# A different order for the four groups of transposes inside each slot of a fused scan kernel

## The reference

```python
proj = xn @ W_in.T;  x, gate = split(proj)            # 2048 channels each
x = silu(conv4(x));  dt, B, C = projections of x      # 16 states per channel
state = state * exp(dt * A) + (dt * x)[..., None] * B # for each token
y = einsum('bdn,bn->bd', state, C)                    # sum over the 16 states
s = ((y + x * D) * silu(gate)) @ W_out.T
g = silu(qlinear(silu(qlinear(xn, gate)) * qlinear(xn, up), down))
out = x_in + s * g
```

## Time and profile before

| | |
|---|---|
| median of 3 runs | 2763.37 us (2761.09 to 2766.05) |
| profiled execution, its own time | 2765.08 us |
| profiled execution, span | 2763.3 us |
| TensorE busy | 2658.4 us (96%) |
| VectorE busy | 2402.0 us (87%) |
| ScalarE busy | 1584.3 us (57%) |
| GpSimd busy | 1982.7 us (72%) |
| granted TensorE clock, mean | 0.99 |

### The profile page before, as it was taken

One profiled execution on the slowest core, in us unless ns is written; L12 is line 12 of the kernel. 1 busy time (PEld: TensorE's weight loads), 2 busy tenths in 40 slices (PEclk: granted clock), 3 DMA queues, 4 the chain that ended last, 5 costly groups with the idle time before them and its releaser, 6 DMA issues.

```text
span 2763.3 us, 41632 instructions
## 1 busy us (share of the span) xinstructions
PE 2658.4 (96%) x14980; PEld 1530.1 (55%) x14980; DVE 2402.0 (87%) x2914; ACT 1584.3 (57%) x2643; POOL 1982.7 (72%) x943
## 2 busy tenths in 40 slices
PE   6999999799999999999999999989999998999999
PEld 3545555355555555555555555556666665555644
DVE  5988877699999998888888888899999999999920
ACT  4454645666666667777776776654555555445500
POOL 2311223288999988889897988788889888999811
PEclk9999999999999999999999999999999999999999
DMA  7755477255555545454544444665555658667541
GB/s 250 235 179 193 134 272 205 101 164 193 162 172 174 168 125 166 130 161 123 170 129 142 139 143 132 180 200 117 158 150 127 162 129 243 169 178 190 150 127 57
DMA packets 338797, 449.09 MB, mean 163 GB/s; under 512 B 170592, under 2 KB 181088, under 8 KB 334496
## 3 DMA queue, kind: packets, MB, share of 16 engines
q1 hardware_dynamic: 338592, 446.43, 54.8%
HBM read 312.39 MB, written 133.96 MB: 162 GB/s over the span
## 4 chain that ended last, share of the span: by engine, by line
PE 35%; DVE 28%; issue 11%; POOL 3%; DMA 3%; ACT 1%; DVEq 0%; SPq 0%; POOLq 0%; ACTq 0%
DVE inj L1517 15%; DVE ysum L1535 9%; PE main_bank L1745 6%; PE main_bank L1747 6%; PE xtp_turned L1703 6%; PE main_bank L1821 4%; PE misc_bank L1747 3%; PE misc_bank L1745 3%; PE misc_bank L1821 2%; DMA h_s<-work 2%; POOL inj L1653 2%; DVE work L1569 1%; DMA gs_s<-work 1%; PE main_bank L1756 1%; DVE us L1544 1%
## 5 line engine op out<-in xcount | busy, mean ns | idle before, releaser
L1653 POOL TENSOR_TENSOR inj<-dd,bb 128x2048 f32<-128x2048 f32 x255 | 1156.1, 4534 | 235.3 <-PE xtp_turned L1703 233.5
L1703 PE MATMUL xtp_turned<-ident,inj 128*128 128x128 f32 x4096 | 628.6, 277 | 45.1 <-DVE inj L1517 34.7
L1517 DVE TENSOR_TENSOR_SCAN inj<-ssm_decay,carry,inj 128x512 f32<-128x512 f32 x512 | 656.4, 1282 | 2.5 <-ACT ssm_decay L1377 2.4
L1517 DVE TENSOR_TENSOR_SCAN inj<-main_decay,carry,inj 128x512 f32<-128x512 f32 x512 | 653.6, 1277 | 0.5 <-ACT main_decay L1377 0.3
L1703 PEld LDWEIGHTS xtp_turned<-ident,inj 128*128 128x128 f32 x4096 | 504.4, 142 | 261.2 <-DVE inj L1517 91.7
L1535 DVE SCALAR_TENSOR_TENSOR ysum<-xtp_turned,cT,ysum 128x512 f32<-128x512 f32 x721 | 534.4, 741 | 99.8 <-PE xtp_turned L1703 98.6
L1377 ACT ACTIVATE main_decay<-dd,aneg 128x512 f32<-128x512 f32 x511 | 351.2, 687 | 381.4 <-DVE inj L1517 381.1
L1377 ACT ACTIVATE ssm_decay<-dd,aneg 128x512 f32<-128x512 f32 x511 | 352.6, 690 | 307.7 <-DVE inj L1517 306.3
L1745 PE MATMUL main_bank<-xx,work 128*128 128x512 f16 x936 | 356.8, 381 | 2.5 <-ACT work L1390 2.5
L1747 PE MATMUL main_bank<-xx,work 128*128 128x512 f16 x936 | 356.7, 381 | 0.0
L1665 POOL TENSOR_TENSOR ysum<-ysum,work 128x512 f32<-128x512 f32 x239 | 306.5, 1282 | 10.5 <-ACT work L1415 10.5
(11 more groups left out here) (206 smaller groups left out, 3930.3 us busy)
## 6 DMA issues: line engine op xcount, KB each, us to landing
bb<-bt_s SPq DMA_DIRECT2D x128, 512.0 KB, 6.0
work<-w_s SPq DMA_DIRECT2D x48, 512.0 KB, 3.8
work<-in_gu_q SPq DMA_DIRECT2D x88, 256.0 KB, 3.4
h_s<-work SPq DMA_DIRECT2D x88, 256.0 KB, 3.8
u_s<-inj SPq DMA_DIRECT2D x64, 256.0 KB, 4.5
dd<-dt_s SPq DMA_DIRECT2D x32, 512.0 KB, 8.8
gs_s<-work SPq DMA_DIRECT2D x64, 256.0 KB, 6.1
us<-u_s SPq DMA_DIRECT2D x60, 256.0 KB, 5.3
```

What stands on the lines that cost most here:

```text
L1517: v.tensor_tensor_scan(inj[:, s % RING, j, :], decay[j % 2][:, :], inj[:, s % RING, j, :], carry[:, step % G * J + j, n:n + 1], ALU.mult, ...
L1653: pool.tensor_tensor(inj[:, e % RING, :, :], dub[:, step % 2, :, :], bb[:, e % 8:e % 8 + 1, :].broadcast_to([P, J, T]), ALU.mult).then_inc ...
L1703: mm = pe.transpose(turned[t % 2][:, j * P:(j + 1) * P], inj[:, s % RING, j, t * P:(t + 1) * P], ident[:, :])
```

## The change

The groups of transposes of a slot are made in the order of token tiles 0, 3, 1, 2 instead of 0, 1, 2, 3 (`ORDER`); `turn(s, q)` now takes a position q, and the bank is `turned[q % 2]`. The places of the four groups in TensorE's program stay. VectorE's places in its own program stay too: `add_up(s-1,1)` now waits for the third group (q = 2) and `add_up(s-1,2)` for the fourth (q = 3). ScalarE's `weigh(s-1)` moves from behind `exp(s+1,0)` to ahead of `exp(s,3)` and waits for the second group. GpSimd's addition of `ev` moves ahead of the products of its iteration. TensorE waits for `weigh` ahead of the fourth group, and `y_back` moves from ahead of the third group to behind it.

```diff
+ORDER = (0, 3, 1, 2)
 def weigh(s):
-    act.wait_ge(s_turn, LEAD + s * TPC + TPC)
+    act.wait_ge(s_turn, LEAD + s * TPC + ORDER.index(ADDS) + 1)
...
-    act.activation(... turned[ADDS % 2] ...)
+    act.activation(... turned[ORDER.index(ADDS) % 2] ...)
 # ScalarE, slot s
+    if s:
+        weigh(s - 1)
     exp(s, 3)
...
-    if s:
-        weigh(s - 1)
     exp(s + 1, 1)
 # VectorE, add_up(s, t)
-    v.wait_ge(s_turn, LEAD + s * TPC + t + 1)
+    q = ORDER.index(t)
+    v.wait_ge(s_turn, LEAD + s * TPC + q + 1)
 # VectorE, after the loop
-for t in range(TPC):
+for t in ORDER:
     add_up(SLOTS - 1, t)
 # GpSimd, iteration e: the addition of ev of slot e-4 (s_acc) stands
 # ahead of the products of slot e (s_inj) instead of behind them
 # TensorE
-def turn(s, t):
-    if t == 0:
+def turn(s, q):
+    t = ORDER[q]
+    if q == 0:
         pe.wait_ge(s_scan, LEAD + s * J + J)
-    if t == 1:
-        atleast(pe, s_ev, s)
-    elif t:
-        pe.wait_ge(s_sum, LEAD + s * ADDS + t - 1)
-    else:
+        atleast(pe, s_sum, s * ADDS - 1)
+    if q == 1:
         atleast(pe, s_sum, s * ADDS)
+    if q == 2:
+        pe.wait_ge(s_sum, LEAD + s * ADDS + 1)
+    if q == 3 and s < SLOTS - 1:
+        pe.wait_ge(s_ev, LEAD + s + 1)
...
 # TensorE, slot s
     piece(1)
-    y_back(...)            # every fourth slot
     down_rank(odd y)
     turn(s - 1, 2)
+    y_back(...)
```

More of the change, by code:

```diff
@@ L1414, in weigh @@
                             atleast(act, s_acc, step * (N - 1) + n - 1)
-                        act.activation(ysum[:, step % 2, ADDS, :] if n == 0 else ev[:, :], turned[ADDS % 2][:, :],
+                        act.activation(ysum[:, step % 2, ADDS, :] if n == 0 else ev[:, :], turned[ORDER.index(ADDS) % 2][:, :],
                                        ACT.Copy, scale=cT[:, step // G * TPC + ADDS, n:n + 1]).then_inc(s_ev, 1)
@@ L1528, in add_up @@
                                 atleast(v, s_yt, (step - 1) * J)
-                            v.tensor_scalar(dst, turned[t % 2][:, :], weight, None, ALU.mult).then_inc(s_sum, 1)
+                            v.tensor_scalar(dst, turned[q % 2][:, :], weight, None, ALU.mult).then_inc(s_sum, 1)
                         else:
@@ L1534, in add_up @@
                                 v.wait_ge(s_acc, LEAD + step * (N - 1) + n - 1)
-                            v.scalar_tensor_tensor(dst, turned[t % 2][:, :], weight, dst, ALU.mult, ALU.add
+                            v.scalar_tensor_tensor(dst, turned[q % 2][:, :], weight, dst, ALU.mult, ALU.add
                                                    ).then_inc(s_sum, 1)
@@ L1641, in _ @@
                             pool.tensor_tensor(wol[:, :], wor[:, :], woh[:, :], ALU.subtract).then_inc(w_lo, 1)
+                        step, n = divmod(e - 4, N)
+                        if 0 <= e - 4 < SLOTS - 1 and n:
+                            pool.wait_ge(s_ev, LEAD + e - 4 + 1)
+                            pool.tensor_tensor(ysum[:, step % 2, ADDS, :], ysum[:, step % 2, ADDS, :], ev[:, :],
+                                               ALU.add).then_inc(s_acc, 1)
                         if (0 < e < SLOTS):
@@ L1661, in _ @@
                                                    ).then_inc(s_dub, 1)
[L1662 to L1666, removed]
                         k = e - 4 - FF0
@@ L1692, in _ @@
                 def _(pe):
-                    def turn(s, t):
-                        if t == 0:
+                    def turn(s, q):
+                        t = ORDER[q]
+                        if q == 0:
                             pe.wait_ge(s_scan, LEAD + s * J + J)
-                        if t == 1:
-                            atleast(pe, s_ev, s)
-                        elif t:
-                            pe.wait_ge(s_sum, LEAD + s * ADDS + t - 1)
-                        else:
-                            atleast(pe, s_sum, s * ADDS)
+                            atleast(pe, s_sum, s * ADDS - 1)
+                        if q == 1:
+                            atleast(pe, s_sum, s * ADDS)
+                        if q == 2:
+                            pe.wait_ge(s_sum, LEAD + s * ADDS + 1)
+                        if q == 3 and s < SLOTS - 1:
+                            pe.wait_ge(s_ev, LEAD + s + 1)
+                        if q == 3 and s == SLOTS - 1:
+                            pe.wait_ge(s_sum, LEAD + s * ADDS + 2)
                         for j in range(J):
-                            mm = pe.transpose(turned[t % 2][:, j * P:(j + 1) * P],
+                            mm = pe.transpose(turned[q % 2][:, j * P:(j + 1) * P],
                                               inj[:, s % RING, j, t * P:(t + 1) * P], ident[:, :])
@@ L1856, in _ @@
                         piece(1)
[L1857 to L1860, removed]
                         for y in scale_halves(s):
@@ L1865, in _ @@
                             turn(s - 1, 2)
+                        y_step, j = at_back(s, 0)
+                        if y_step is not None:
+                            atleast(pe, d_hal, sum(h <= s for h in HA_SLOT))
+                            y_back(y_step, j, back)
                         if ffn(k):
```

## The result

The changed kernel takes 2899.98 us, median of 4 runs (2897.73 to 2905.29), against 2762.23 for the kernel before, measured beside it. The ratio is 1.0496, 95% interval 1.0483 to 1.051. The forecast was 2885, range 2860 to 2910. The profiled execution spans 2897.8 us, 134.5 more than the 2763.3 of before.

A forecast was written before the change was run, and what follows sets the result against it. VectorE was taken to bound the gate, down and output stages, TensorE the FFN stage. Loops between them add 37.7 + 36.8 + 1 + 44.9 + 1 = 121.4 us to the median 2763.4, giving 2885 us, range 2860 to 2910.

The forecast's parts named there:

- What bounds which stage: VectorE sets the pace in gate, down and output stages, TensorE in the FFN stage at 9.35 us a slot.
- half the sum: Rival: late slots catch up or TensorE runs its third group earlier, so only half the loss shows; 2824 us, chance 0.06.
- The loop through the third group: VectorE's second addition waits for the third group, closing a loop through TensorE and VectorE: 8.02 us a plain slot.
- The loop through the fourth group where `y_back` stands ahead of it: VectorE's third addition waits for the fourth group: 7.90 us a slot, 8.34 with `y_back`, where it decides.
- A result or a silu inside the loop costs its whole 0.60 us: Output and down stages: such work between second addition and third scan lengthens the loop from 8.02 to 8.62 us.
- The four slots of the down stage: Four repeating slots take 8.62, 8.62, 8.02 and 7.54 us, +2.54 together; 14.5 times, +36.8 us.
- ScalarE and the fourth group's wait for `weigh`: Gate stage: `weigh` ends near T0+4.3 (T0: first group's start), fourth group starts at T0+5.25; cost 0, 0.9 us of cover.
- The FFN stage at cost 0 and +1: Loop of 8.34 us stays below TensorE's 9.35 a slot, so cost 0; +1 us for slots with late ScalarE work.
- The start of the down stage, +1: Slots 148 to 155, where the stage starts up unevenly, were taken to lose 1 us.
- the clock down: Rival: TensorE's idle time ahead of each T0, its first group's start, halves its clock; 62 us more, 2947 us, chance 0.05.
- The rival of a loss in the FFN stage: `weigh` waits behind the FFN's ScalarE work and the fourth group for it; 0.5 us a slot, +44, 2929 us, chance 0.07.
- Faster by GpSimd: Rival: addition fills GpSimd's wait, `weigh` no longer late; output stage's 2.4 us and FFN idle time go; 2751 us, chance 0.02.

The follow-up runs named there:

- waits_alone: Kernel before with only VectorE's second and third additions waiting for the third and fourth groups, and `y_back` behind the third group; 2897.89 us, ratio 1.0472.
- order_0132: Changed kernel with token tiles in order 0, 1, 3, 2: second addition waits for the second group again, `weigh` for the third; 2887.93 us, ratio 1.0436.
- back_ahead: Changed kernel with `y_back` ahead of the third group of transposes again, except in slot 155; 2912.75 us, ratio 1.0531.
- early_groups: Changed kernel with the third group of transposes right behind the second and the fourth one piece of the matrix product sooner; 2765.92 us, ratio 1.0007.
- adds_later: Changed kernel with VectorE's second addition behind scan(s,2) and its third behind scan(s,3); 2759.81 us, ratio 0.9977, and 2759.51 us, ratio 0.9978, when repeated.

## Why the prediction was right, and where it was off

- **What bounds which stage.** Right. The three stages where VectorE was full grew, by 36.7, 36.2 and 44.7 us; waits_alone shows that the waits, with `y_back` in its new place, do it without the rest of the change. Not one slot caught up, as half the sum would have needed: from fourth scan to fourth scan every plain slot of the gate stage takes 7.98 to 8.00 us.
- **The loop through the third group.** Right in mechanism and size: 7.99 us measured, 8.02 forecast. The handed-over time of 0.04 us and the group's end 0.60 us after its start held (815.55 to 815.59), so the lower bound of 25 us was not needed. TensorE's idle time ahead of T0 reads 0.84 us in such a slot, not 1.1, since the row counts it from the modelled end of the last matmul.
- **The loop through the fourth group where `y_back` stands ahead of it.** Right: 8.33 measured, 8.34 forecast; order_0132 (8.32 with `y_back`, 7.89 without, computed 8.34 and 7.90) and back_ahead (8.42, computed 8.46) bear it out.
- **A result or a silu inside the loop costs its whole 0.60 us.** Right: 8.58, forecast 8.62, and order_0132, where it is outside, takes 13.9 us less in the output stage.
- **The four slots of the down stage.** Right one by one: 8.66, 8.59, 8.10 and 7.51 us measured, 8.62, 8.62, 8.02 and 7.54 forecast. So their sum is no luck of errors that cancel.
- **ScalarE and the fourth group's wait for `weigh`.** Right in the gate stage by early_groups, which asks for the group even sooner and loses nothing.
- **The FFN stage at cost 0 and +1.** Mis-sized: +10.5. "The addition waits about 0.8 us, but VectorE had waited 1.10 us at each T0; the wait moves" holds for the loop: VectorE's waits for transposes were 95.8 us in 88 cases before and 92.6 in 178 after. It does not hold for what hangs on VectorE in between. h, the fourth scan and ScalarE's work behind them can come later, up to the scaling for which TensorE's low-rank matmul waits; that this is the path is argued, the wait at its end is measured. That wait rose from 7.4 us in 6 cases to the first row below, and all of TensorE's waits from 9.9 to 16.5 us. waits_alone has 11.2 us of it and 6.6 of the 10.5, so about that part comes from VectorE's lateness. Some 2 us more is TensorE's clock (see the rivals). TensorE's longest waits in the FFN stage after:

```profile
PE main_bank L1762 <- ACT main_bank L1446: 12.6, 7, 4.2
PE main_bank L1751 <- ACT work L1391: 3.1, 1, 3.1
```

- **The start of the down stage, +1.** Mis-sized: +5.1. Its slots were not worked out singly, though the loops were to be had: slots 151 and 152 take 8.33 and 7.98 us from fourth scan to fourth scan, as in the other stages, and took 7.36 and 7.33 before. waits_alone has the loss (77.3 us), early_groups (65.8) and adds_later (66.5) have none of it, so it is the two waits again.
- **Sum.** 121.4 forecast, 134.5 between the profiles and some 138 between the medians. Between the profiles that is 13.1 us more than forecast; the two mis-sized terms are 13.6 too low and all the rest together 0.5 too high.
- **The rivals.** The loops did not bring the clock down: the granted clock is 1.00, 0.99, 1.00 and 0.99 in the four stages, and idle times up to 1.44 us ahead of T0 in every second slot of the output stage left TensorE at its 2.4 GHz level. In the FFN stage, where TensorE waited longer in single slots, it did fall. After 4.19 us of idle time the 2.4 us from 1713.6 on read 0.50, the 1.2 GHz level, and matmuls started 0.43 us apart instead of 0.22. The kernel before has such places too: after 2.44 us of idle time ahead of 1516.56, the clock read 0.50 from 1517.9 to 1521.1. By the granted clock of 4 us slices the stage ran 5.1 us longer for it before and 6.9 after, an estimate that gives the clock about 2 of the 10.5 us. The rival of a loss in the FFN stage came true by a quarter in size (10.5 of 44) but not in mechanism: TensorE waited nowhere in that stage for `weigh`. "Faster by GpSimd" was wrong for this kernel; whether its 2.4 us are part of what adds_later gained is not shown.

What stays open: the 4 us of the FFN stage beyond waits_alone, and where the 6 us of adds_later come from.

## What to carry to other kernels

Where two engines hand work to each other in every round, write down for each hand-over when it is ready and when it is due, both from the start of the round. A reordering that makes one ready later than due can close a loop. Each round then takes the time to the late hand-over plus all that stands between it and the release of the next round, though no engine is full any more. Move the consumer by as much as the producer: here the new order alone cost 5% and with the two additions a scan later it gained 0.2%.

A wait that only moves within slack can still make late what stands behind it; follow it through every in-order queue, the one that issues transfers above all.

## What the runs showed that I had not expected

- SP's queue couples engines that share no data: a conversion on ScalarE that came later held the store of h behind a load and cost 22 us of the FFN stage (853.5 against 831.1), and products that came later on GpSimd held the store of the gate and cost most of the 57 us that the gate stage lost (480.3 against 423.0).
- Two halves that each cost time gave a gain together: the change as it stands +5.0%, the later additions alone +1.1%, both -0.2%.
